# Adding all tiles' rows of the first experts to one tensor, each scatter behind the landing of the preceding one

## The reference, cut to what matters

```python
x = x + L0_attn(layernorm(x))
x = x + L0_ffn(layernorm(x))      # 16 experts, the best 2 for each row
x = x + L1_attn(layernorm(x))     # latent projections, rotary embedding, softmax attention
x = x + L1_ffn(layernorm(x))      # 64 experts, the best 8 for each row
```

## Time and profile before

| | us |
|---|---|
| median of 3 runs (lowest to highest) | 4341.45 (4338.65 to 4342.63) |
| profiled execution, its time | 4355.53 |
| profiled execution, its span | 4353.7 |
| first scatter of the first experts starts | 335.97 |
| last scatter of the first experts starts | 620.25 |
| first load of the projection is issued | 627.27 |
| attention's first loads are issued | 923.58 |

### The profile page before, as it was taken

One profiled execution on the slowest core, in us unless ns is written; L12 is line 12 of the kernel. 1 busy time (PEld: TensorE's weight loads), 2 busy tenths in 40 slices (PEclk: granted clock), 3 DMA queues, 4 the chain that ended last, 5 costly groups with the idle time before them and its releaser, 6 DMA issues. The chain is left out here.

```text
span 4353.7 us, 55023 instructions
## 1 busy us (share of the span) xinstructions
PE 3908.7 (90%) x17786; PEld 2972.2 (68%) x17786; DVE 3607.6 (83%) x4517; ACT 2636.2 (61%) x3523; POOL 2214.4 (51%) x1837
## 2 busy tenths in 40 slices
PE   7949967739999999999999999999999999989563
PEld 4635535527888888888888888888888888867321
DVE  7845547749999999999999999999999999947511
ACT  6613333316777777777777777777777777732221
POOL 2547755644555555555555555555555555520163
PEclk9969988869999999999999999999999999989776
DMA  7213446663222232223322232222322233046396
GB/s 266 60 45 62 65 108 201 213 178 63 54 60 50 56 79 52 59 49 68 66 57 54 50 82 55 60 50 57 78 52 58 49 70 65 17 151 213 90 244 159
DMA packets 351954, 388.13 MB, mean 89 GB/s; under 512 B 141772, under 2 KB 279825, under 8 KB 339123
## 3 DMA queue, kind: packets, MB, share of 16 engines
q1 hardware_dynamic: 327606, 358.28, 32.5%
q0 software_dynamic: 24064, 26.32, 3.6%
HBM read 236.66 MB, written 117.79 MB: 81 GB/s over the span
## 5 line engine op out<-in xcount | busy, mean ns | idle before, releaser
L1556 POOL TENSOR_TENSOR at_pl<-at_pf,at_ph 128x512 fp32r<-128x512 f32 x1024 | 1330.6, 1299 | 1341.3 <-ACT at_ph L1703 1340.9
L1702 ACT ACTIVATE at_pf<-at_ps_s 128x1024 f32<-128x1024 f32 x1024 | 1050.7, 1026 | 745.8 <-PE at_ps_s L1752 745.8
L1619 DVE TENSOR_TENSOR at_pl<-at_pf,at_ph 128x512 fp32r<-128x512 f32 x1024 | 1356.0, 1324 | 20.6 <-ACT at_ph L1703 20.6
L1601 DVE TENSOR_REDUCE at_mx<-at_ps_u 128x2 f32<-128x1024 f32 x1024 | 1250.1, 1221 | 22.5 <-PE at_ps_u L1736 22.5
L1703 ACT ACTIVATE at_ph<-at_ps_s 128x1024 fp32r<-128x1024 f32 x1024 | 1042.2, 1018 | 0.0
L1752 PE MATMUL at_ps_s<-at_q,at_k 66*128 66x512 f32 x2048 | 819.7, 400 | 0.0
L1751 PE MATMUL at_ps_s<-at_q,at_k 128*128 128x512 f32 x2048 | 811.3, 396 | 0.6 <-ACT at_ph L1703 0.6
L1768 PE MATMUL at_ps_v<-at_ph,at_vh 128*128 128x512 f32 x2048 | 809.1, 395 | 0.2 <-POOL at_pl L1556 0.2
L1770 PE MATMUL at_ps_v<-at_pl,at_vh 128*128 128x512 f32 x2048 | 809.2, 395 | 0.0
L1769 PE MATMUL at_ps_v<-at_ph,at_vl 128*128 128x512 f32 x2048 | 808.1, 395 | 0.0
L1736 PE MATMUL at_ps_u<-at_k,at_qp 128*128 128x512 f32 x2048 | 647.5, 397 | 64.5 <-DMA at_q<-at_low 48.7
(11 more groups left out here) (257 smaller groups left out, 4023.2 us busy)
## 6 DMA issues: line engine op xcount, KB each, us to landing
at_k<-kT SPq DMA_DIRECT2D x64, 512.0 KB, 10.1
at_q<-qT SPq DMA_DIRECT2D x64, 512.0 KB, 9.1
wgu<-Wgu_in SPq DMA_DIRECT2D x64, 384.0 KB, 6.6
qT<-pj_rot SPq DMA_DIRECT2D x32, 512.0 KB, 3.2
vT<-pj_vo SPq DMA_DIRECT2D x32, 512.0 KB, 4.4
kT<-pj_rot SPq DMA_DIRECT2D x32, 512.0 KB, 3.1
at_raw<-qT SPq DMA_DIRECT2D x32, 512.0 KB, 4.9
at_raw<-kT SPq DMA_DIRECT2D x32, 512.0 KB, 6.8
```

Of the source, the lines that this page charges most:

```text
L1556: pool.tensor_tensor(pl[:, n % NP, at], pf[:, n % NP, at], ph[:, n % NP, at].bitcast(F32), ALU.subtract).then_inc(s["pl2_ready"], 1)
L1601: dve.tensor_reduce(mx[:, qb % 2, 2 * i:2 * i + 2], ps_u[:], X, ALU.max).then_inc(s["u_max"], 1)
L1619: dve.tensor_tensor(pl[:, n % NP, at], pf[:, n % NP, at], ph[:, n % NP, at].bitcast(F32), ALU.subtract)\
L1702: act.activation(pf[:, n % NP], ps_s[:, n % 2], ACT.Exp, scale=DH ** -0.5)
```

## The change

`x_odd` goes. All tiles of the first experts are added to `x_acc`. Each scatter waits for the landing of the scatter one tile earlier instead of two tiles. In POOL's list the gather of tile i + 6 now stands ahead of this wait and of the scatter of tile i, where it stood behind the scatter. The zeros for `x_odd` (four DMAs), its four loads in the projection and the four additions on DVE are gone.

```diff
@@ build, linear_attention
-        self.x_odd = nc.dram_tensor("x_odd", (T, D), F32)
...
-                for acc in (self.x_odd, self.out_odd):
-                    for n in range(0, NT, 8):
-                        sp.dma_start(acc[:].rearrange("(n p) d -> p n d", p=P)[:, n:n + 8], xr[:]).then_inc(s["zeroed"], 16)
+                for n in range(0, NT, 8):
+                    sp.dma_start(self.out_odd[:].rearrange("(n p) d -> p n d", p=P)[:, n:n + 8], xr[:]).then_inc(s["zeroed"], 16)
...
-                        act.wait_ge(s["zeroed"], 16 * 2 * NT // 8)
+                        act.wait_ge(s["zeroed"], 16 * NT // 8)
@@ experts
-        targets = (self.x_acc[:], self.x_odd[:])
...
                 for i in range(N):
                     pool.wait_ge(s["ys_ready"], i + 1)
-                    if i > 1:
-                        pool.wait_ge(*scattered(i - 2))
-                    pool.indirect_dma_start(targets[i % 2], rows(i), y[:, i % RY], None, bounds_check=T - 1,
-                                            oob_is_err=False, compute_op=ALU.add).then_inc(s[f"scat{i % 2}"], 16)
                     if i + AHEAD < N:
                         gather(i + AHEAD)
+                    if i > 0:
+                        pool.wait_ge(*scattered(i - 1))
+                    pool.indirect_dma_start(self.x_acc[:], rows(i), y[:, i % RY], None, bounds_check=T - 1,
+                                            oob_is_err=False, compute_op=ALU.add).then_inc(s[f"scat{i % 2}"], 16)
@@ project
-            xo = sb("xo", [P, 2, QT, D])
...
-                    sp.dma_start(xo[:, q % 2], odd[:, part]).then_inc(s[f"x{q}"], 16)
...
-                    part, p = slice(q * QT, (q + 1) * QT), q % 2
-                    dve.wait_ge(s[f"x{q}"], 32)
-                    link(dve.tensor_tensor(x[:, part], x[:, part], xo[:, p], ALU.add))
+                    p = q % 2
+                    dve.wait_ge(s[f"x{q}"], 16)
```

More of the change, by code:

```diff
@@ L358, in _ @@
                 sp.wait_ge(s["bias_out"], 16)
-                sp.wait_ge(s["zeroed"], 16 * 2 * NT // 8)
+                sp.wait_ge(s["zeroed"], 16 * NT // 8)
                 sp.wait_ge(s["experts_in"], 48 * E)
@@ L1133, in project @@
             acc = self.x_acc[:].rearrange("(n p) d -> p n d", p=P)
-            odd = self.x_odd[:].rearrange("(n p) d -> p n d", p=P)
             def heads_of(dram):
```

## The result

| | before | changed |
|---|---|---|
| median of 4 runs each (lowest to highest), us | 4342.04 (4338.65 to 4343.51) | 4403.96 (4400.31 to 4411.33) |
| profiled execution, its time, us | 4355.53 | 4411.33 |
| profiled execution, its span, us | 4353.7 | 4409.5 |

The changed kernel takes 1.0146 times as long (95% interval 1.0133 to 1.0158): 61.9 us more. The forecast was 4416, with 4380 to 4440 as its range.

The account below looks back on a forecast made before the run. The first experts' loop was to be bound by landing and POOL's release instead of PE: loop +83.8, tile 0 +1.4, loads -2.7, additions -7.9, together +74.6 on the median 4341.45, giving 4416 us, range 4380 to 4440.

Parts of the forecast that it names:

- What bounds the loop: First experts' loop: PE's 3.42 us a tile gives way to landing plus POOL's release, 4.77 us a step.
- The size of the loop: First experts: 70 steps of 4.77 and 9 empty ones of 3.8, 368.1 us against 284.3, +83.8.
- The gather ahead of the wait: POOL's list: gather is free inside the landing, otherwise the step is 1.4 us longer; costs +1.4 at tile 0.
- Zeros: First stage: dropping the zero DMAs of `x_odd` gains 0, at most 1 us.
- Loads: Projection start: without `x_odd`'s megabyte on SP, `rope` lands earlier and PE starts 2.7 us sooner; bounds 0 and 5.
- The projection as a whole: Projection: -2.7 from loads and -7.9 from three additions, all on the path; gain of 4 to 15 us allowed.
- A: First experts' loop: release is cheap, only the 0.30 us gap remains, step about 4.27, time 4378; 10%.
- B: First experts' loop: the chain doesn't bind, scatters land within 2.8 us, loop costs nothing, time 4332; 3%.
- C: First experts' loop: PE goes cold after idling in every tile, 5.3 us a tile, time 4453; 5%.
- the forecast's own remark that the clock would drop: PE in the first experts' loop: the clock is expected to drop and the time not to follow.
- D: First experts' loop: landings lengthen by sums on rows just written, step over 5.0, time above 4436; 7%.
- the signs named for the forecast's case: Scatters 4.7 to 4.8 us apart behind a DMA, PE near 75% or slower clock, chunks 0, 2, 4 2.6 us shorter.

Follow-up runs that it names:

- kernel 1: Kernel before, each scatter waiting for the landing of the scatter one tile earlier; two tensors, loads and additions kept: 4438.07 us, +84.4 against before.
- kernel 3: Changed kernel with the gather of tile i + 6 behind the scatter again: 4420.35 us, +66.6 against the kernel before.
- Kernel 4: Changed kernel that still writes the four zero DMAs of `x_odd` and waits for them: 4413.19 us, +59.5 against the kernel before.
- kernel 11: Changed kernel measured again, unaltered, in a later set: 4412.77 us, +63.1 against the kernel before.
- 12: Changed kernel with the gather behind the scatter, measured again in a later set: 4425.52 us, +75.9 against the kernel before.
- 2: Kernel before with the one-tile-earlier wait and all tiles sent to `x_acc`; zeros, loads and additions kept: 4435.75 us, +82.0 against before.
- 10: Changed kernel with the statistics of quarter 1 ahead of DVE's first rotation: 4401.84 us, +52.2 against the kernel before.
- kernel 6: Kernel before without the projection's four additions and four loads from `x_odd`, chain untouched: 4341.66 us, -9.2 against before.
- Kernel 5: Kernel before without the four additions in the projection, loads from `x_odd` kept, chain untouched: 4344.37 us, -6.5 against before.
- 7: Kernel before with quarter 1's addition and statistics moved ahead on DVE, beside chunk 0's preparation: 4340.11 us, -10.8 against before.
- 9: Kernel before with early statistics, quarters 0 and 1 added by DVE, quarters 2 and 3 by accumulating DMAs: 4334.11 us, -15.6 against before.
- kernel 8: Kernel before with early statistics, quarters 1 to 3 of `x_odd` added by POOL's accumulating DMAs, loads of x moved: 4337.02 us, -13.9 against before.

## Why the prediction was right, step by step

**What bounds the loop: right.** That the chain of landing and release takes the loop from PE's 3.42 to near 4.7 us a tile was argued from SP's instruction behind the landing and the second experts' chain. The wait alone (kernel 1) shows it, with everything else as it was: +84.4 us. One row was misread on the way: the 0.82 and 0.90 us of the earlier trace rows are POOL's idle time since the issue to `out_odd` that stands between the two, not since a landing. By the semaphores in the trace the scatter at 4284.70 landed after 3.2 us and the next to the same tensor started 0.83 us behind that. So the step of 4.04 was read rightly, and that 0.82 was also the release is luck.

**The size of the loop: too large by 9 us.** 368.1 us were predicted, 358.7 measured. The landing is 3.83 to 3.85 us in the medians of all kernels with the chain, on one tensor or two, not 3.95; the issue inside it fell from 1.66 to 1.78 us to 1.59, about as much as the landing lost. The release is 0.77 instead of 0.82, so a median step is 4.62 and the mean, with a few long landings, 4.67 instead of 4.77: 70 x 0.10 = 7 us. The empty tiles, priced at 3.8 between 3.43 and 4.77, took 3.53, since a landing with nothing to move still takes 2.7 us: 9 x 0.27 = 2.4 us.

**The gather ahead of the wait: the price at tile 0 right, the reason wrong.** +1.4 was predicted for the first scatter and +1.5 measured. But the text also said that this place makes the gather free and that without it the step would be 1.4 us longer. It lies in the landing from either side: kernel 3 steps by 4.77, not 6. The loop is 7 to 9.5 us shorter all the same with the gather ahead, in two pairs of traces (4 against 3, 11 against 12). Of this some 5 us are a shorter release, which all eight traces show and of which the forecast had nothing; the rest are long landings, which don't follow the order in all traces. What the order does change is how far ahead the gathers run, one tile more: `ex_y` is done some 9 us before its scatter starts, against 4.6 in the kernels 1, 2, 3 and 12.

**Zeros: right.** Kernel 4 can't be told from the changed kernel. The 5.1 us that the first stage is shorter in the profiled execution aren't theirs either: among kernels without the zeros the first `ex_y` comes at 330.1, 336.5, 330.7, 337.6 and 337.0 us (changed, 3, 10, 11, 12), with them anywhere from 332.8 to 338.7 (before and the seven others). It varies from trace to trace.

**Loads: right at the start, and a second place missed.** PE starts 2.86 us earlier against 2.7, and in kernel 6 by 2.94. But "the DMAs of the loads themselves overlap" doesn't hold in chunk 2: there the load of quarter 3 from `x_odd` stands ahead of the first store of q, which POOL waits for, and costs 2.9 us (37.0 or 37.1 us with it, 34.1 without). The forecast had nothing for this.

**The projection as a whole: too small by 8 us in the traces.** -10.6 was predicted, -18.7 is in this trace. The additions were given -7.9, "all on the path". At first sight PE's waits in the projection bear that out, before and then changed:

```profile
PE pj_ps_c L1339 <- ACT pj_hT L1282: 16.7, 4, 5.3
```

```profile
PE pj_ps_c L1332 <- ACT pj_hT L1275: 8.7, 4, 2.6
```

Three of these four waits were 5.2 or 5.3 us and are now 2.6, each by the 2.65 us of an addition. But a shorter wait isn't yet a shorter chunk. Kernel 5 has the same three short waits, and its chunk 2 is as long as before: PE's next wait there is 7.3 instead of 4.2 us, since POOL waits for the store behind the loads. So the sum gave 2.65 us to chunk 2's addition, which was hidden, and nothing to its load, which cost 2.9; that the chunk's total came out is luck. On the path are the additions of chunks 0 and 4.

What the forecast lacked lies in chunk 0 (6.9 us shorter, where 2.7 + 2.6 were given), chunk 4 (36.6 to 30.7) and chunk 5, which holds no addition (30.4 to 27.4). Chunk 0 also moves with PE's clock: in the same code DVE's first rotation comes 32.0 us after the first load in the changed kernel and 30.2 in kernel 11, where the granted clock from 24 to 34 us after the load was 0.68 and 0.93. In chunk 4 part of it is on DVE. After the statistics come eight small instructions with 128 x 8 elements, and most of them take either 0.2 us or 1.2 to 1.3. The timelines of DVE and of POOL in chunk 4 of the changed kernel, and one such pair of before, in its chunk 4:

```profile
863.62 0.17 DVE L1192 TENSOR_TENSOR pj_var<-pj_mv,pj_r 128x8 f32<-128x8 f32 x1
863.82 0.17 DVE L1193 TENSOR_TENSOR pj_var<-pj_var,pj_r 128x8 f32<-128x8 f32 x1
...
866.54 1.29 DVE L1201 TENSOR_TENSOR pj_r<-pj_r 128x8 f32<-128x8 f32 x1
```

```profile
863.99 1.30 POOL L1243 TENSOR_TENSOR pj_rot<-pj_t 128x512 f32<-128x512 f32 x1 [1.82 <-DMA qT<-pj_rot]
...
866.51 1.30 POOL L1243 TENSOR_TENSOR pj_rot<-pj_t 128x512 f32<-128x512 f32 x1
```

```profile
805.49 1.22 DVE L1199 TENSOR_TENSOR pj_var<-pj_mv,pj_r 128x8 f32<-128x8 f32 x1
806.75 1.20 DVE L1200 TENSOR_TENSOR pj_var<-pj_var,pj_r 128x8 f32<-128x8 f32 x1
```

At 863.62 POOL is idle until 863.99, and DVE's instruction takes 0.17 us; at 866.54 it falls on a rotation of POOL that started 0.03 us before, and takes as long as that. All those of over 0.6 us in the projection, in every trace, run while POOL works. (The Trainium skill has this in SBUF — State Buffer, section SBUF: two separate sides: an instruction of VectorE with two inputs in SBUF and one of GpSimd that reads SBUF lock each other out for a whole instruction. The trace agrees.) Before, four of chunk 4's take so long, 5.5 us for all eight; in the changed kernel two, 3.5 us. So 2.0 us hang on where these instructions fall. The kernels 4, 10 and 11 have two long ones and a chunk 4 of 30.7 us, the kernels 3, 6 and 12 four and 32.9 to 34.1. That sorts the lengths of chunk 4; it was not tried by an experiment, and why chunk 5 goes with it (27.4 or 30.3 us in the kernels 11 and 12, of the same projection) stays open. The five kernels with the chain and without `x_odd` in the unchanged order of the projection (changed, 3, 4, 11, 12) have 275.9 to 282.9 us, the three with it (before, 1, 2) 294.0 to 296.3: on average -16.2, not -10.6.

**The rivals.** A (step 4.27) is refuted: 0.77 us of release behind every landing. B (the chain doesn't bind) is refuted by kernel 1; by the figure that the Trainium skill gives for a DMA from GpSimd (DMA: Bandwidth & Descriptors, section Anatomy of one DMA (SWDGE path)) a landing would be an estimated 2.3 us, and these scatters took 3.8. C (PE goes cold) is refuted, and so is the forecast's own remark that the clock would drop: PE now idles for some 0.8 us of each 4.67 (15.6 of 90 us), much of it for the gathers, and its clock stays at 1.00, the 2.4 GHz level, until the empty tiles (0.87 from 655 to 694). D is refuted by kernels 1 and 2. Most of the signs named for the forecast's case came, the sizes aside: idle behind a DMA ahead of the scatters, PE waiting for `ex_xg`, the last scatter 358.7 us behind the first; PE's share fell to 83%, not to 75%. The chunks didn't lose 2.6 us each but 6.9, 2.9 and 5.9.

**The sum.** Of the profiled execution +55.8 was measured where +74.6 was predicted: 9 us are the loop, 8 the projection, 5 the first stage's chance, less 4 of later stages that the change doesn't touch. On the medians it is +61.9, 12 less than the forecast of 4416.

## What to carry to other kernels

A wait for the landing of the DMA just issued makes each step cost issue, landing and release together, here 1.6 + 2.2 + 0.8 = 4.6 us, whatever the engines do; before you take a second target away, read this sum from who else waits for the same semaphore and from another chain in the same trace, and set it against the pace of the engine that bounds the loop. Here that loses 74 us of loop to save some 16 in the next stage, and most of what is saved there (10.8 to 15.6 us, kernels 7 to 9) was to be had by moving additions into time in which DVE waits for PE's first results, or to DMAs, with the loads out of the way of the stores. A load that no one waits for can still cost its time when it stands ahead of a store that someone waits for; so a shorter wait on one engine has to be followed to the end of the stage before it is counted. A gain of a few us in a pipelined stage is also moved by how two engines' instructions fall on each other, so one trace is not enough to read it.

## What the runs showed of the hardware that wasn't expected

- A scatter that has nothing to move (all its rows skipped) still takes 2.7 us from the start of its issue to its landing, against 3.8 for 128 rows of 1 KB.
- Adding to the same DRAM tensor behind a landing is no slower than alternating between two: 3.8 us in both.
- POOL's release is 0.77 us when the gather stands between the two waits and 0.83 when both stand directly ahead of the scatter; eight traces agree.
- In the changed kernel PE idled for 0.8 us in each filled tile's 4.67, and its granted clock stayed at 1.00 from 335 to 655 us (kernels 1 and 12 have 0.98 from 520 to 600), though before a single gap of 1.51 us was followed by matmuls at half the clock.
- A DVE instruction on 128 x 8 elements with two inputs takes 0.17 us, or mostly 1.2 to 1.3 us beside a rotation of POOL.
- A store of q on SP's queue takes 9.7 us from its issue to its landing behind loads of 1 or 2 MB, 6.2 with no load ahead in the chunk (kernel 8), and most later ones 3.0 to 3.2.
- An accumulating DMA of 1 MB into SBUF costs POOL 1.6 us of issue.
